# Flamingo block on one core: products of probabilities and values moved to the ends of steps 5 and 11

## What is computed

```python
# x: 16 x 224 x 512, context: 16 x 750 x 512, 16 heads of 32, 8 experts of 512 -> 2048 -> 512
q = (layernorm(x) @ Wq.T).reshape(B, L, H, D) * scale
k = (ctx @ Wk.T).reshape(B, -1, H, D)
v = (ctx @ Wv.T).reshape(B, -1, H, D)
scores = sigmoid(einsum('blhd,bshd->bhls', q, k))
o = einsum('bhls,bshd->blhd', scores, v).reshape(B, L, E)
x = x + tanh(g_xattn[0]) * (o @ Wo.T)
h = gelu(einsum('etd,edf->etf', layernorm(x) by expert, w1) + b1)
x = x + tanh(g_ffn[0]) * (einsum('etf,efd->etd', h, w2) + b2)
```

## Time and profile before

| | us | busy |
|---|---|---|
| median of 3 runs | 1655.48 | |
| the profiled execution's own time | 1653.71 | |
| its span | 1652.0 | |
| TensorE (PE), products | 1644.5 | 100% |
| TensorE, weight loads (PEld) | 1452.0 | 88% |
| VectorE (DVE) | 804.8 | 49% |
| ScalarE (ACT) | 796.9 | 48% |
| GpSimd (POOL) | 175.9 | 11% |

### The profile page before, as it was taken

How to read it: one execution, slowest core, us unless ns; L and a number is a source line. 1 busy time by engine, 2 the same in 40 slices (tenths; PEclk the granted TensorE clock), 3 DMA queues, 4 the chain that set the end, 5 groups by cost and what they waited for, 6 DMA issues and landing times.

```text
span 1652.0 us, 30322 instructions
## 1 busy us (share of the span) xinstructions
PE 1644.5 (100%) x11460; PEld 1452.0 (88%) x11460; DVE 804.8 (49%) x1388; ACT 796.9 (48%) x1087; POOL 175.9 (11%) x261
## 2 busy tenths in 40 slices
PE   9999999999999999999999999999999999999999
PEld 8888888888888888888888887999999999999998
DVE  5545444443443443544443443674746565555544
ACT  6655555555555555555555556333333333333332
POOL 1212111111111111111121120000000000000000
DMA  8977687777677787786776775535344352526251
GB/s 278 265 216 217 198 222 204 195 226 206 192 220 213 194 224 204 193 237 187 210 225 186 210 227 149 203 125 180 124 168 150 131 183 98 188 93 227 94 171 48
DMA packets 195691, 309.03 MB, mean 187 GB/s; under 512 B 27088, under 2 KB 153616, under 8 KB 195568
## 3 DMA queue, kind: packets, MB, share of 16 engines
q1 hardware_dynamic: 173632, 229.43, 49.4%
q0 software_dynamic: 21936, 77.94, 13.6%
HBM read 228.44 MB, written 78.84 MB: 186 GB/s over the span
## 4 chain that ended last, share of the span: by engine, by line
PE 97%; DMA 2%; DVE 0%; SPq 0%; ACT 0%; issue 0%; POOLq 0%; DVEq 0%; ACTq 0%
PE fill_ps L686 31%; PE scores_ps L872 19%; PE fill_ps L853 14%; PE scores_ps L728 10%; PE heads_ps L745 9%; PE fill_ps L695 6%; PE heads_ps L853 5%; PE fill_ps L696 3%; DMA k_st<-k_scr 1%; DMA k_scr<-k_stage 0%; DMA probs<-WKT_in 0%; DMA part_scr<-part 0%; PE scores_ps L695 0%; SPq L404 0%; PE scores_ps L696 0%
## 5 line engine op out<-in xcount | busy, mean ns | idle before, releaser
L872 PE MATMUL scores_ps<-ctx_hl,wK 128*128 128x448 f32 x1536 | 316.6, 362 | 0.0
L872 PEld LDWEIGHTS scores_ps<-ctx_hl,wK 128*128 128x128 f32 x1536 | 288.1, 188 | 19.8
L686 PE MATMUL fill_ps<-ctx_hl,wK 128*128 128x500 f32 (+1 forms) x1560 | 287.6, 334 | 0.4 <-DVE wK L1093 0.4
L686 PE MATMUL fill_ps<-wV,ctx_hl 128*125 128x512 f32 x1152 | 280.5, 395 | 0.2 <-DVE k_stage L1201 0.2
L686 PEld LDWEIGHTS fill_ps<-ctx_hl,wK 128*128 128x128 f32 x1560 | 236.2, 189 | 31.8 <-issue 6.0
L686 PEld LDWEIGHTS fill_ps<-wV,ctx_hl 128*125 128x125 f32 x1152 | 208.9, 186 | 48.1 <-DVE k_stage L1201 0.4
L853 PE MATMUL fill_ps<-wQ,wV 128*128 128x448 f32 x1152 | 243.4, 365 | 0.0
L853 PEld LDWEIGHTS fill_ps<-wQ,wV 128*128 128x128 f32 x1152 | 216.0, 188 | 17.2 <-issue 0.4
L911 ACT ACTIVATE probs<-scores_ps 125x896 f32<-125x896 f32 x192 | 176.8, 921 | 86.7 <-PE scores_ps L728 54.4
L728 PE MATMUL scores_ps<-q_st,k_st 96*125 96x224 f32 x1536 | 200.7, 273 | 2.1 <-DMA k_st<-k_scr 2.1
L728 PEld LDWEIGHTS scores_ps<-q_st,k_st 96*125 96x125 f32 x1536 | 188.0, 188 | 16.0 <-issue 6.2
(11 more groups left out here) (120 smaller groups left out, 1706.1 us busy)
## 6 DMA issues: line engine op xcount, KB each, us to landing
k_st<-k_scr SPq DMA_DIRECT2D x576, 125.0 KB, 3.9
v_sb<-w_in SPq DMA_DIRECT2D x92, 512.0 KB, 4.6
k_scr<-k_stage POOLq DMA_DIRECT2D x62, 500.0 KB, 4.5
ctx_raw<-ctxT_in SPq DMA_DIRECT2D x48, 500.0 KB, 4.6
q_st<-q_scr SPq DMA_DIRECT2D x192, 112.0 KB, 4.0
k_scr<-k_stage POOLq DMA_DIRECT2D x68, 250.0 KB, 4.1
probs<-w_in SPq DMA_DIRECT2D x32, 512.0 KB, 3.6
q_scr<-q_stage POOLq DMA_DIRECT2D x64, 224.0 KB, 5.0
```

Of the source, the lines that this page charges most:

```text
L686: last = pe.matmul(out_, lhsT(kt, a), rhs(kt, c), start=(kt == 0 and t == 0), stop=(kt == KT - 1 and t == 2))
L872: last = pe.matmul(y_ps[:, dt, 0:T], w2[:, slot, a, k, dt * P:(dt + 1) * P], hid_hl[:, slot, d, k, :], start=(c == 0 and k == 0 and t == 0 ...
```

## The change

Behind the change both calls of `heads` stand at the end of a step, behind its fills: h = 0 at step 5, h = 1 at step 11. Both fall ahead of the next scores. The fills are spread anew: ("K", 0) moves from step 1 to step 0, ("V", 0) from 8 to 6, ("Q", 1) from 9 to 8, ("V", 1) from 10 to 11, and ("K", 11), ("Q", 2) and ("Q", 3) from 11 to 10. In batch 0 ("K", 5) moves from 5 to 6. The first keys' products are ordered by the operands that they need. The first context piece of item 1 is loaded in batch -1, `load_w1(0, 1)` stands a step later in SyncE's queue, and the first hidden products of expert 0 a step earlier. No product is added or dropped.

```diff
-    FILL = [(1, "K", 0), (1, "O", 0), (1, "O", 1), (2, "O", 2), (2, "O", 3), (3, "K", 2), (3, "V", 2), (4, "K", 3), (4, "V", 3), (5, "V", 4),
-            (5, "V", 5), (6, "K", 5), (7, "K", 6), (7, "Q", 0), (8, "V", 0), (8, "K", 8), (9, "K", 9), (9, "Q", 1),
-            (10, "V", 1), (11, "K", 11), (11, "Q", 2), (11, "Q", 3)]
+    FILL = [(0, "K", 0), (1, "O", 0), (1, "O", 1), (2, "O", 2), (2, "O", 3), (3, "K", 2), (3, "V", 2), (4, "K", 3), (4, "V", 3),
+            (5, "V", 4), (5, "V", 5), (6, "K", 5), (6, "V", 0), (7, "K", 6), (7, "Q", 0), (8, "K", 8), (8, "Q", 1),
+            (9, "K", 9), (10, "K", 11), (10, "Q", 2), (10, "Q", 3), (11, "V", 1)]
...
-    FILL_0 = [(0, "K", 0), (1, "V", 5), (2, "K", 2), (3, "Q", 7), (4, "K", 3), (5, "K", 5), (7, "K", 6), (7, "V", 0),
-              (8, "Q", 0)] + [f for f in FILL if f[0] > 7 and f[1:] != ("V", 0)]
+    FILL_0 = [(0, "K", 0), (1, "V", 5), (2, "K", 2), (3, "Q", 7), (4, "K", 3), (6, "K", 5), (7, "K", 6), (7, "V", 0),
+              (8, "Q", 0), (8, "K", 8), (9, "K", 9), (9, "Q", 1), (10, "K", 11), (10, "Q", 2), (10, "Q", 3), (11, "V", 1)]
...
-    W_LO = {0: (2,), 4: (3,), 6: (4,), 10: (5,), 12: (6,), 13: (7,)}
+    W_LO = {-1: (2,), 4: (3,), 6: (4,), 10: (5,), 12: (6,), 13: (7,)}
...
-    HIDDEN_AT = {7: [(0, 0, 0)], 8: [(0, 0, 1), (0, 1, 0)], 9: [(0, 1, 1), (1, 0, 0)], 10: [(1, 0, 1)],
+    HIDDEN_AT = {6: [(0, 0, 0)], 7: [(0, 0, 1)], 8: [(0, 1, 0), (0, 1, 1)], 9: [(1, 0, 0)], 10: [(1, 0, 1)],
                  12: [(2, 0, 0), (2, 0, 1)]}
...
-                    if known(b, B - 1) and s == 5:
+                    if known(b, B - 1) and s == 6:
                         load_w1(0, 1)
...
-                    if attends(b) and prepares(b) and s in (1, 2, 5):
-                        load_ctx(b + 1, nh, npar, {1: 0, 2: 1, 5: 2}[s])
+                    loads = {1: 1, 5: 2} if known(b, 0) else {1: 0, 2: 1, 5: 2}
+                    if attends(b) and prepares(b) and s in loads:
+                        load_ctx(b + 1, nh, npar, loads[s])
+                    if known(b, -1) and s == 3:
+                        load_ctx(1, 0, 1, 0)
...
+            def first_keys(out_):
+                for t, (a, d, ready) in enumerate(((HI, HI, s_ctx_hi), (HI, LO, s_ctx_lo), (LO, HI, s_w_lo))):
+                    pe.wait_ge(ready, 1)
+                    if t == 0:
+                        pe.wait_ge(s_w_hi, 1)
+                    for kt in range(KT):
+                        last = pe.matmul(out_, w["K"][:, a, kt, 0:P], ctx_hl[:, 0, d, kt, :], start=(t == 0 and kt == 0),
+                                         stop=(t == 2 and kt == KT - 1))
+                return last
...
-                    if s == 0 and follows(b):
-                        heads(b - 1, 1 - par, 1)
-                    if s == VISIT and attends(b):
-                        heads(b, par, 0)
                     for kind, i in fills_at(b, s):
                         fill(b, kind, i)
+                    if s in (VISIT - 1, STEPS - 1) and attends(b):
+                        heads(b, par, s // VISIT)
```

More of the change, by code:

```diff
@@ L761, in fill @@
                     c, mt = step_of(i) % 3, step_of(i) // 3
-                    if mt == 0:
+                    if mt == 0 and not (known(b, -1) and i == 6):
                         pe.wait_ge(s_ctx_lo, 3 * n + c + is_pair(b, i) + 1)
-                    if known(b, -1) and i == 6:
-                        pe.wait_ge(s_w_lo, 1)
                     if known(b, 0) and i == 0:
                         pe.wait_ge(s_w_lo, 6)
-                    if is_pair(b, i):
+                    if known(b, -1) and i == 6:
+                        last = first_keys(ps[:, 0:SC])
+                    elif is_pair(b, i):
                         last = three_terms(ps[:, 0:2 * SC], lambda kt, a: w["K"][:, a, kt, mt * P:(mt + 1) * P],
@@ L978, in body @@
                 for s in range(STEPS):
+                    if s == 0 and follows(b):
+                        o_hi(b - 1, 1)
+                    if s == VISIT and attends(b):
+                        o_hi(b, 0)
                     if attends(b):
@@ L983, in body @@
                             square(b, which)
[L984 to L987, removed]
                     for kind, i in fills_at(b, s):
@@ L1227, in body @@
                         o_lo(b, 0)
+                    if known(b, -1) and s == 0:
+                        for n in W_LO[-1]:
+                            w_lo(n)
                     for kind, i in fills_at(b, s):
```

## The result

| | before | after |
|---|---|---|
| median | 1655.02 us (6 runs) | 1661.33 us (6 runs, 1660.83 to 1663.28) |
| profiled execution's own time | 1653.71 | 1660.83 |
| its span | 1652.0 | 1659.2 |

The changed kernel is slower: ratio 1.0038, 95% interval 1.0028 to 1.0049. The forecast was 1663.6, 1.0049 of 1655.48.

What follows compares the result with a forecast made beforehand. TensorE, busy for 1644.5 of 1652.0 us, was taken to bound the kernel. 11.2 for the wait, less 0.45 (start), 0.75 (batch 0) and 1.9 (batch 15), gave +8.1 on 1655.48: 1663.6 us, range 1658.5 to 1669.5.

Steps and rivals of the forecast that it cites:

- The wait: Step 5, 14 batches: heads directly behind ("V", 5) wait for ScalarE's copy, 0.80 us each, 11.2 in all (9.7 to 13.0).
- the hand-over: From the end of ScalarE's copy to the start of heads: 0.14 us, taken from VectorE's hand-over to the first fill.
- The bound without any hand-over: Heads at step 5 start the moment the copy of ("V", 5) ends: a wait of 0.69 us per batch.
- the turn: Switching TensorE into or out of heads: about 0.1 us, the same from a value tile as from scores; one hidden by the wait.
- Batch 0: Scores of step 6 come over 3 us later, behind heads, and find their gathered keys: gain 0.75 us (0.3 to 0.8).
- Batch 15: Gather for step 8's scores leaves some 7 us earlier, ahead of the expert's weights: gain 1.9 us (0.9 to 2.0).
- The start: First fill no longer waits for VectorE's split of the key weights: gain 0.45 us (0 to 0.6).
- The moves costed at nothing: Steady batches: the moved fills and other moves cost 0; moved fills keep at least two steps, 7 us or more, before their reader.
- A covered wait: Rival, chance 0.14: heads behind ("V", 5) do not wait, only the end gains of 3.1 us remain, 1652.4 us.
- second wait: Rival, chance 0.07: the new spread makes keys late in each of 14 steady batches, adding 10.9 us, 1674.5 us.
- The clock: Rival, chance 0.02: TensorE's clock falls to 1.2 GHz behind each of 14 waits, 65.5 us more, 1729 us.
- The sum: Whole kernel: 11.2 - 0.45 - 0.75 - 1.9 = +8.1 us, with bounds of +6.3 and +11.8.

Runs made afterwards that it cites:

- the kernel with the wait at its reader: Changed kernel, same order of products, but heads wait for the sixth value tile only before the first product that reads it: median 1650.54 us, ratio 0.9973.
- two small edits: Changed kernel with the sixth tile's wait moved to its first reader, 1650.54 us; or with ("K", 5) moved from step 6 to step 5, 1650.65 us.
- the doubled copy: Changed kernel with ScalarE copying ("V", 5) twice and counting it only after the second copy: one time of 1670.92 us, span 1669.2.
- The kernel with the load back at step 5: Changed kernel with load_w1(0, 1) back at step 5 of SyncE's queue, ahead of batch 15's gather for step 8: one time of 1663.82 us.

## Why the prediction was right, and where it was off

**The wait.** Right in kind and place: 14 waits of heads for ScalarE's copy, 0.7 us each. Forecast 0.80 per batch, measured 0.72, in all 10.0 against 11.2. What was mis-sized is the hand-over. I took it near 0.14, from VectorE to the first fill; here it is 0.05 behind the copy. The bound without any hand-over, 0.69, was the nearer end: 0.69 and 0.05 make the 0.74 that the table shows against the kernel with the wait at its reader, and the steady batch of that kernel is 0.02 shorter than that of the kernel before. That ScalarE would be free at that moment held (it had idled 2.21 us again), and so did the turn: heads behind ("V", 1) at step 11 cost no more than behind scores. The rule of the Trainium skill on tiling modes (TensorEngine Tiling (Array Packing), Key Properties), which is that a change of mode drains the array, fits this too: the turn of 0.1 lay inside the wait, as heads began 0.05 behind the copy's end, and 0.74 and not 0.84 was lost.

**Batch 0.** Forecast -0.75, measured -0.67. The scores find their keys.

**Batch 15.** Forecast -1.9, measured -2.11. Two runs from both sides show that the order of the two loads is the cause: with the loads as before 2.6 are lost, and with that line alone the stretch takes 22.55 us, against 22.60 in the changed kernel.

**The start.** Here a step failed: "Gain 0.45" (its lower bound of 0 held). The first fill did start 0.48 earlier, but ("V", 2) gave 0.39 of it back. In the chain it waits for VectorE's half of the keys before it, these for a place in `k_stage`, and that for the store of the first keys, 11.70 to 19.45. I looked at the first fill's operands and not at who is late next. In nine executions with the new order of the first keys, ("V", 2) began between 19.83 and 21.29, on average at 20.50; in four with the old one between 20.50 and 20.78, on average at 20.58. A gain can't be told from that spread. One sum of this step was wrong without harm: eight of the first fill's twelve products take two thirds of 1.39 us, not half, so the low weights were due at about 8.7 and not at 8.4.

**The moves costed at nothing.** They cost nothing in the changed kernel, but my reason for ("K", 0) was too thin. I wrote that the lightest step is 3.4 us and never asked what heads themselves had covered. Moving heads takes a cover from the copy, and also from the sigmoids of step 0; the second would have cost 17 us, had ("K", 0) not taken their place. That the term came out at nothing was luck as far as the reason goes.

**The rivals.** A covered wait did not come by itself, but two small edits make it, and then the times are 1650.5 and 1650.7, some 4.4 below the kernel before, where that case had 3.1. No second wait appeared in a steady batch. The clock stayed at the 2.4 GHz level through all 14 waits, and also through those of 1.3 us of the doubled copy: one clock record of 1.00 reaches from 6.04 to 1658.09 us in the changed kernel and from 7.02 to 1669.31 in that one, and heads behind a wait take the same 4.68 us. The Trainium skill's case of a clock that goes back and forth with brief idling (TensorE: Matmul & The Clock Gate, A second HAM failure mode) is not this one.

**The sum.** 10.0 - 0.09 - 0.67 - 2.11 = 7.1, against 8.1 forecast. The medians differ by 6.3 and the profiled executions by 7.1; the before side's lay 1.3 under its median, the after side's 0.5.

## What to carry to other kernels

Before moving a block in an engine's order, ask what it stands behind and what it stands between: the work ahead of it may cover another engine's copy of its operands, and the block itself may cover the engine that reads what came before. Where TensorE is busy for the whole span, an uncovered copy of half a microsecond costs its full length in every round, 0.74 us here. The cheapest mend here was not to move work but to move the wait, from the head of the block to the first instruction that reads the late operand.

In a queue with waits of its own, a load that waits for compute holds back those behind it. Put it behind the loads that are due first, as one line in batch 15 showed (2.6 and 2.1 us, in two kernels).

## What was not expected of the hardware

The 36 turns of the identity at the start, the same instructions with nothing to wait for, took between 5.53 and 6.96 us in these executions. How many of them fall in a stretch of 2 us shows where the time goes. The kernel with the load back at step 5, where they took 6.96, then the kernel before, where they took 6.08:

```profile
3.60:5.60 2.00, 2.00 (x12) 2.00 (x11) 0.14 (x1) 1.02 (x1) 0.00 (x0) 1.00 1.03 419
5.60:7.60 2.00, 2.00 (x12) 2.00 (x11) 1.84 (x2) 1.64 (x2) 0.00 (x0) 1.00 1.02 418
...
3.60:5.60 2.00, 2.00 (x12) 2.00 (x11) 0.12 (x1) 1.03 (x1) 0.00 (x0) 1.00 1.03 415
5.60:7.60 2.00, 2.00 (x19) 1.90 (x17) 1.89 (x2) 1.67 (x2) 0.00 (x0) 1.00 1.03 424
```

In every execution the turns start 0.21 us apart at first and 0.11 us apart later. Only the moment of the step differs: after 14 turns in the fastest execution, after 27 in the slowest. The view prints a granted clock of 1.00 for all of it, but that number does not cover the slow turns: eleven of the thirteen traces hold a clock record of 1.00, and it begins just at the step, at 4.53 us in the fastest, 6.04 in the changed kernel and 7.46 in the one above. Half the rate ahead of it is what the level of 1.2 GHz against that of 2.4 GHz would give. So the start begins at the lower level whatever the kernel, and the step comes at another time in each execution; why it moves is not shown, since TensorE had done nothing but turns in all of them.

With the first keys waiting for their high halves alone, the first fill follows the turns directly and began between 7.16 and 8.37 us in nine executions. With the old order it mostly waited for the weights' split and began between 8.12 and 8.38 in four. A change of a few tenths at the start can't be judged from one execution.
